# Laying out anew the merge order of eight work streams in a one-core decoder-layer kernel

## The reference

```python
x = layernorm(x + attn(x, Wqkv, Wo))                 # 16 heads of 128, 2 kv heads, rotary,
                                                     # 30*tanh(logits/30), causal, softmax, @ Wo
x = layernorm(x + xattn(x, ctx, mask, wq..bo))       # 16 heads of 16 against ctx (256 tokens);
                                                     # x and the weights quantised to whole
                                                     # numbers for the q and output projections
x = layernorm(x + ffn(x, Wr, br, W1, W2))            # softmax router, best 4 of 16 blocks of 64,
                                                     # h = gelu(x @ W1.T) * mask; h @ W2.T
```

## Time and profile before

| what | value |
|---|---|
| runs of the kernel | 413.67, 414.06 and 414.71 us, median 414.06 |
| the profiled execution | 413.82 us, its span 412.1 us |
| PE busy | 381.5 us, 93% of the span |
| DVE, ACT, POOL busy | 315.3, 246.8 and 151.4 us |
| granted TensorE clock | 0.998 over the span |

### The profile page before, as it was taken

How to read it: one execution, slowest core, us unless ns; L and a number is a source line. 1 busy time by engine, 2 the same in 40 slices (tenths; PEclk the granted TensorE clock), 3 DMA queues, 4 the chain that set the end, 5 groups by cost and what they waited for, 6 DMA issues and landing times.

```text
span 412.1 us, 9281 instructions
## 1 busy us (share of the span) xinstructions
PE 381.5 (93%) x3144; PEld 327.1 (79%) x3144; DVE 315.3 (77%) x924; ACT 246.8 (60%) x528; POOL 151.4 (37%) x173
## 2 busy tenths in 40 slices
PE   3889899999999989998999999999999989899895
PEld 3768769888899868687898778989869877668794
DVE  4998798367676868888887788688778888777653
ACT  5355642536638894476789356678974256994240
POOL 6488545738645123453422325231113320000101
PEclk9999999999999999999999999999999999999999
DMA  7993435553255313242241612220123000000000
GB/s 224 328 372 107 149 102 150 196 171 92 70 173 162 97 28 77 63 118 78 77 130 41 166 32 46 79 78 25 29 78 104 1 2 14 14 3 2 13 14 27
DMA packets 21134, 38.45 MB, mean 93 GB/s; under 512 B 2528, under 2 KB 11616, under 8 KB 21088
## 3 DMA queue, kind: packets, MB, share of 16 engines
q1 hardware_dynamic: 20272, 37.06, 29.6%
q10 hardware_dynamic: 816, 0.79, 0.6%
HBM read 25.52 MB, written 5.24 MB: 75 GB/s over the span
## 4 chain that ended last, share of the span: by engine, by line
PE 64%; DVE 17%; issue 7%; ACT 6%; POOL 3%; DMA 2%; SPq 0%; DVEq 0%; POOLq 0%; ACTq 0%
PE bank L452 12%; PE acc L539 8%; PE bank L625 6%; PE bank L692 5%; PE bank L677 5%; PE bank L483 5%; PE bank L506 4%; PE bank L614 3%; ACT xs L831 3%; PE bank L565 3%; PE bank L637 2%; PE bank L520 2%; PE bank L491 2%; PE bank L509 2%; DVE wqkv_lo L918 2%
## 5 line engine op out<-in xcount | busy, mean ns | idle before, releaser
L831 ACT ACTIVATE xs<-xs,xneg 128x256 f32<-128x256 f32 x128 | 54.3, 500 | 13.4 <-DVE xneg L1089 13.1
L1248 POOL TENSOR_TENSOR a_lo<-a_flat,a_hi 128x512 fp32r<-128x512 f32 x32 | 41.9, 1311 | 30.2 <-ACT a_flat L752 30.2
L452 PE MATMUL bank<-x_hi,wqkv_hi 128*128 128x256 f32 x144 | 45.6, 317 | 7.3 <-DVE wqkv_lo L918 7.3
L1237 POOL TENSOR_TENSOR q_T<-q_T,rope_s 128x512 f32<-128x512 f32 x24 | 31.1, 1301 | 54.7 <-DMA rope_s<-rope_t 54.4
L539 PE MATMUL acc<-wo_s,a_hi 128*128 128x256 f32 x256 | 50.1, 294 | 1.1 <-POOL a_lo L1248 1.1
L1266 POOL TENSOR_TENSOR rstd<-var_eps,half 128x1 f32<-128x1 f32 x24 | 13.2, 551 | 99.2 <-DVE var_eps L976 99.2
L1089 DVE CUSTOM_DVE_ANT_0 xs<-bank,mask_s 128x256 f32<-128x256 f32 x128 | 46.1, 419 | 1.7 <-PE bank L614 1.6
L506 PE MATMUL bank<-v_s,p_near 128*128 128x129 f32 x256 | 41.6, 277 | 1.5 <-POOL p_far L1255 1.1
L539 PEld LDWEIGHTS acc<-wo_s,a_hi 128*128 128x128 f32 x256 | 39.3, 189 | 3.3 <-POOL a_lo L1248 1.8
L452 PE MATMUL bank<-x_lo,wqkv_hi 128*128 128x256 f32 x144 | 41.3, 287 | 0.0
L452 PE MATMUL bank<-x_hi,wqkv_lo 128*128 128x256 f32 x144 | 41.1, 285 | 0.0
(11 more groups left out here) (152 smaller groups left out, 954.2 us busy)
## 6 DMA issues: line engine op xcount, KB each, us to landing
wo_s<-wo_parts SPq DMA_DIRECT2D x24, 512.0 KB, 3.4
rope_s<-rope_t SPq DMA_DIRECT2D x54, 128.0 KB, 2.3
wo_parts<-wo_s SPq DMA_DIRECT2D x8, 512.0 KB, 3.1
stage<-in_wqkv SPq DMA_DIRECT2D x5, 512.0 KB, 4.5
xs<-in_wo SPq DMA_DIRECT2D x8, 256.0 KB, 3.8
y<-in_x SPq DMA_DIRECT2D x4, 256.0 KB, 2.9
ctx_s<-in_ctxT SPq DMA_DIRECT2D x4, 256.0 KB, 3.1
mask_s<-in_mask SPq DMA_DIRECT2D x4, 256.0 KB, 2.9
```

Source lines behind the costliest of these rows:

```text
L452: ins = mm(ps, lhs[i], rhs[j], start=(k == 0 and n == 0), stop=(last and n == 2))
L831: activation(xs[:, t, m, m2, :], xs[:, t, m, m2, :], ACT.Exp, bias=xneg[:, t, m, m2:m2 + 1], scale=-1.0)\
L1237: g.tensor_tensor(dst, dst, (rope_s if b else rope_t)[:, n % 2], ALU.add).then_inc(sig["rotated", 0], 1)
L1248: g.tensor_tensor(a_lo[:, j % 2], a_flat[:, j % 2], a_hi[:, j % 2].bitcast(F32), ALU.subtract)\
```

## The change: the string ORDER

Only the string changes. Each letter occurs as often as before (m 148, x and y 108 each, s 48, r 45, c 28, n and o 24 each), so each stream has the same operations in the same order, with the same instructions, semaphore waits and buffers; what changes is how the streams are merged.

```diff
 ORDER = (
-    "rrrrrrrmmrsrrssmmrrmsrmmssrmmrsmmmmmmscsmmmmcsmmmrmcmmssmmrrcccmmmmmrrsmmmmmcmssmrrcmmmmmrmmmssmsmrrrmccy"
-    "mssmmmmsxsmmmyxmmxssrmmmxymmmmmmmmxxmymmrrxyxmxxmmmyymsxyyxxxryrxxyyyxxxymyxyyxsxyyxyyyxxssrrymymmmxmyssc"
-    "scmmmxrssxccccrrmmyxmmxsnmmyxmmsxsxymmmxxmmmmxxryxnyrxxnnymmyymmmxxyyymryyxxxyyxyyyxryyroyxxoyymmyxmyxxcc"
-    "ssmmxossrrmmymxsmsmxccnmmmxysrccmoyxoymmyxmsxmnxxymxssxyooyxxxyxxyrxyymxxxnxyyyxxmyxyyymnxyyyyxmyyysyxosy"
-    "xymmmmmmyxmmmmynmmccmmmmnccccynoxoyoxyxnnyxyxoyxyxxoxyxynyxyyyxyxyyyxyxxyxyxxyyxxxoyxnoyxxynnxoyxnonynoon"
-    "onnoooon")
+    "rrrrrrrrmrssmsrmmsrmmmrmssmrrmmmmmrmrsssmmmmmsmmmmsscrmcmmmcmmmmrrccmmmmmmmrrcssmmmmssmrrcmmmmycssmrrmmmm"
+    "mxsssccmmryxmmmmssysrrmmmmmmxmymmyxryymmmmxxymyrrxyxxxmyxxyyymmmmssssyxxxrrxxxxmmmmxyyyxxyyxsysyryxxccmmx"
+    "smmmxxcsysccmmmymxcrrnxmmymmsmmmyssrmyxmmmxnymmrxxmnymmxnyxxxyrrxxyyxmyxoyyroyxxxsxyyymmyxyyxysxymmyxsyy"
+    "xxroycmcnxmyxxccccsssynxroyxmmmmmoyxsmmmxsyoxxysxxxymxxmxmyxxmynrxxxymoxyyyryyxyyxxmyyoyxsyyyssxxmnyyymmx"
+    "mmxmymmymymmcmmycmmmcmxocccyonnonyxxynxnyxyooyyyxxyyxxyxyyxyxxxxyyyyxxxxyyxxxyyoxyxnoxoynnxynxnonyynoon"
+    "onnoonoo")
```

More of the change, by code:

```diff
@@ L135 @@
 ORDER = (
-    "rrrrrrrmmrsrrssmmrrmsrmmssrmmrsmmmmmmscsmmmmcsmmmrmcmmssmmrrcccmmmmmrrsmmmmmcmssmrrcmmmmmrmmmssmsmrrrmccy"
-    "mssmmmmsxsmmmyxmmxssrmmmxymmmmmmmmxxmymmrrxyxmxxmmmyymsxyyxxxryrxxyyyxxxymyxyyxsxyyxyyyxxssrrymymmmxmyssc"
-    "scmmmxrssxccccrrmmyxmmxsnmmyxmmsxsxymmmxxmmmmxxryxnyrxxnnymmyymmmxxyyymryyxxxyyxyyyxryyroyxxoyymmyxmyxxcc"
-    "ssmmxossrrmmymxsmsmxccnmmmxysrccmoyxoymmyxmsxmnxxymxssxyooyxxxyxxyrxyymxxxnxyyyxxmyxyyymnxyyyyxmyyysyxosy"
-    "xymmmmmmyxmmmmynmmccmmmmnccccynoxoyoxyxnnyxyxoyxyxxoxyxynyxyyyxyxyyyxyxxyxyxxyyxxxoyxnoyxxynnxoyxnonynoon"
-    "onnoooon")
+    "rrrrrrrrmrssmsrmmsrmmmrmssmrrmmmmmrmrsssmmmmmsmmmmsscrmcmmmcmmmmrrccmmmmmmmrrcssmmmmssmrrcmmmmycssmrrmmmm"
+    "mxsssccmmryxmmmmssysrrmmmmmmxmymmyxryymmmmxxymyrrxyxxxmyxxyyymmmmssssyxxxrrxxxxmmmmxyyyxxyyxsysyryxxccmmx"
+    "smmmxxcsysccmmmymxcrrnxmmymmsmmmyssrmyxmmmxnymmrxxmmnymmxnyxxxyrrxxyyxmyxoyyroyxxxsxyyymmyxyyxysxymmyxsyy"
+    "xxroycmcnxmyxxccccsssynxroyxmmmmmoyxsmmmxsyoxxysxxxymxxmxmyxxmynrxxxymoxyyyryyxyyxxmyyoyxsyyyssxxmnyyymmx"
+    "mmxmymmymmymmcymmycmmmcmxocccyonnonyxxynxnyxyooyyyxxyyxxyxyyxyxxxxyyyyxxxxyyxxxyyoxyxnoxoynnxynxnonyynoon"
+    "onnoonoo")
 def work_streams():
```

## The result

The new order runs in 399.64 us (four runs, 399.34 to 399.87), the old one on the same chip in 414.38 (four runs, 413.67 to 415.51): ratio 0.9641, 95% interval 0.9617 to 0.9666. The direction was right, the size was not.

A forecast was written before the change was run, and what follows sets the result against it. PE was taken as the busiest engine, with some 40.8 us idle or thin that an order could change; 2.0 (start) + 1.6 (middle) - 0.3 (before last batch) = 3.3 us off 413.82, forecast 410.6, range 405.5 to 416.8.

The forecast's parts named there:

- The start: Up to about 66 us: less PE idle time in the new order, 2.0 us won, bounds 0 to 3.5.
- The walk along the queues: Operation-by-operation timing of the start: proj(0, 0) at 34.7 us, ctx(0, 0) at 61.2, PE idle 7.05 us instead of 9.5.
- Rival 1: POOL limits the start: its 2.0 us are gone, and with the middle halved 413 to 414.5 us; chance 0.16.
- The middle: From 60 us to the last norm1: fewer tight pairs, 1.6 us won, between 4.5 won and 1 lost.
- shortfall of tight pairs: Dense PE work missing between dependent operations against a fixed way through other engines: 5.1 us old, 1.9 new.
- The halving: Only half of the middle's 3.2 us was credited, as a tight pair costs nothing where PE has waited already.
- rival 2: The whole of the middle is won: 2.4 + 4.5 us, giving some 407 us; chance 0.18.
- The stretch before the last batch: 319 to 343 us, DVE without a gap: 0.3 us lost, between 0.7 won and 0.9 lost.
- The end itself: Last 15 operations: one move, ffn(3, t0) ahead of hidden(3, 1, t1), cost 0, at most some 0.3 us.
- Rival 3: DVE falls behind at batch 2's change-over, PE pays 4.3 us or more, 417 us; chance 0.22 with other such bursts.

The follow-up runs named there:

- e1: New order for its first 84 operations, up to the second norm1 of batch 0, then the old order: 410.93 us, ratio 0.9907 to the old kernel.
- e4: Old order with 14 operations moved, most by one to four places, at eleven waits seen in its trace: 413.38 us, ratio 0.9983 to the old kernel.
- e9: Old and new orders merged by position, streams x and y placed as in the new, all others as in the old: 442.93 us, ratio 1.0694.
- e7: New order with three xmix and turn_q(1, 0) moved forward so that their pairs are tight: 409.96 us, ratio 0.9877 to the old kernel.
- e8: Old order with only the move for its largest middle wait, at turn_q(1, 0): 414.16 us, ratio 1.0001 to the old kernel.
- e5: Old order with POOL's a_lo replaced by two writes of about the same time that read nothing: 411.25 us, ratio 0.9923.
- e16: Old order with each cross-attention exponential on ACT done on half its columns: 409.83 us, ratio 0.9890 to the old kernel.
- e14: New order with turn_ox(3, t1) moved ahead of hidden(2, 1, t1) and route(3, t1) ahead of turn_m(3, t0): 400.39 us, ratio 0.9646 to the old kernel.
- e13: Order of e4 given to PE and the bank rotation alone, other engines on the old order: 416.88 us, ratio 1.0041 to the old kernel.
- e2: Old order up to the two norm1 of batch 0, then the new order: 405.14 us, ratio 0.9770 to the old kernel.
- e3: New order up to ctx(2, 1), then the old order: 404.70 us, ratio 0.9759 to the old kernel.
- e11: Old order with six PSUM banks instead of seven: 426.73 us, ratio 1.0272 to the old kernel.
- e12: New order with six PSUM banks instead of seven: 407.92 us, ratio 0.9823 to the old kernel.
- e10: Old and new orders merged by position, streams x and y placed as in the old, all others as in the new: 436.66 us, ratio 1.0533.
- e6: New order with POOL's a_lo replaced by two writes of about the same time that read nothing: 399.81 us, ratio 0.9644 to the old kernel.
- e15: As e14, with near(1, 2) also moved behind val(1) and turn_x(3, t0) ahead of hidden(1, 1, t0): 401.12 us, ratio 0.9663 to the old kernel.

## Why the prediction was right or wrong

**The start: right in mechanism, short by 1 us.** It was forecast at 2.0 us within 0 to 3.5; the lag shows 3.0 at position 66, and e1, which has the new start alone, won 3.8 between medians. The walk along the queues held. PE in order of time, kernel after:

```profile
34.90 0.48 PE L539 MATMUL acc<-wo_s,a_hi 128*128 128x256 f32 x2
...
60.04 1.88 PE L565 MATMUL bank<-wkv_s,ctx_s 128*128 128x512 f32 x4
```

proj(0, 0) was forecast at 34.7 and came at 34.90, where the old order has it at 38.42; `quant_w`, forecast at 46.2, came at 46.54; ctx(0, 0), forecast at 61.2, came 1.2 us sooner. turn(0, 7), put at 14.8 us behind dense work counted from the start of the span, came at 66.37, 12.8 behind (in the old order's trace it is 16.7, where I put 16.1), so what I let go back there (0.8 us behind two `ctx`) did not. Instead 1.1 us go back at near(1, 2), which stands still for POOL's sum at 77.9 us and which my walk did not reach. Rival 1, POOL as the limit of the start, is refuted by the stretch 24 to 38 us: POOL has 12.51 us of work in 14 and PE no gap.

**The middle: this is the step that failed.** "Counted between 60 us and the last `norm1`" the shortfall of tight pairs fell from 5.1 to 1.9 us and I credited 1.6; 9.9 us came, or 11.0 counted up to just ahead of turn_k(3, 0). The halving was not the main fault, since even the full count (4.5 with what hangs on it, rival 2) is less than half. The failed step is that a shortfall, dense work between two operations set against one fixed way for each kind of pair, stood for the time that PE waits. It errs both ways. For the old middle it gives 5.1 us where PE's visible waits alone sum to 7.0 and its lag grows by 14.3. For the new one it leaves 1.9 us, 1.7 of them from `turn` to `proj`, where the trace has no visible wait at all: proj(2, 0), with 2.67 us of dense work where I said that 3.76 were needed, started 3.17 us behind the start of its `turn`, and the lag grew by 0.15 us there.

The measure does not rank orders either: e4 has the smallest shortfall of all and the old order's time, e9 a smaller one than the old and 28.5 us more. What it leaves out is what stands ahead of a pair's work in the queues between. e7 showed 2 us of DVE's other work ahead of a `query`, e8 a norm that stands in DVE's queue for POOL's root, e9 banks held 3.8 and 3.4 us by a reader that was late; by the lag, the part of the collisions that e5 took away is about 1 us of the old middle, and the part of ACT's exponentials that e16 took away about 1.5. My text had the evidence for a larger term: it noted that the waits of the old middle sum to about 10 us, and then let their shortfall of 5 stand for them. The new order leaves PE no visible wait in the middle; that it would do so could not be read from the pairs.

**Single waits do not tell what an order can win.** The prediction costed pair by pair. The traces of e8 and e14 show waits taken away at their place and others in their stead within some microseconds, and the times of e4 and e13 show no gain from 14 moves. e1, e2 and e3 show that whole stretches do keep their gain.

**The stretch before the last batch: right.** turn_k(3, 0) was to stand still for 1.7 us with the later waits shrinking in exchange, 0.3 us lost in all, between 0.7 won and 0.9 lost. PE in order of time, kernel after:

```profile
313.45 0.63 PE L595 MATMUL bank<-ident_s,parts 128*128 128x128 f32 x4 [0.96 <-DVE parts L1047]
```

It waits 0.96 us, and the lag grows by 1.1 us there. From just ahead of it to the end the new order wins about 0.3 us, within the bounds; the 1.4 us of the table leave this loss out, as they start behind it. The end itself was forecast at 0 and is: the last `ffn` to the end takes 4.8 us against 4.7.

**Rival 3, DVE behind at batch 2's change-over, is refuted.** turn_k(2, 0), at 238.2 us, does not wait; the new kernel's PE has 59.00 of 59 us in that stretch. The burst of DVE work that I counted is there, but the operation that it was to hold up is on time; how much slack DVE had when it entered was not read.

**What stays open.** Of the 9.9 to 11 us of the middle, e5 and e16 give two shares in the old order, each by itself: 3.1 for a part of the collisions over the whole kernel (about 1 of it in the middle, by the lag) and about 1.5 for a fifth of ACT's exponentials. They are floors, not the whole of either. The visible waits give 1.0 us to banks and 6.0 to operands; how the rest of the 11 us divides between DVE's queue, POOL's queue and the banks was not separated, and e11 and e12 say only that the old order is the more sensitive to the banks. That the lateness of the queues as a whole made the old middle is thus shown at single places and argued for the sum. A kernel with DVE's work cut without changing its order was not tried.

## What to carry to other kernels

When in-order engines share one merged order, read its worth from the lag of the bottleneck engine behind its own dense work, stretch by stretch, and take as the upper bound of the gain the whole lag that a stretch adds, not the shortfall of its dependent pairs. A pair with nothing between costs (e7), but a loose one may wait as well, as its way is as long as the queues on it, and a wait mended at its place may come back at the next one. Judge a new order as a whole, and walk the queues of all engines for the stretches that bind (the walk of the start was good to about a microsecond in 60). Two orders joined end to end kept the gain of each stretch here (e1, e2, e3); the same two woven together stream by stream cost 5 to 7% (e9, e10).

## What the runs showed of the hardware

- DVE's two-operand add and its cast take 0.43 us alone and 1.30 to 1.38 beside POOL's two-operand sums. The Trainium skill (SBUF — State Buffer, section Who interferes with whom) makes a DVE instruction with two SBUF inputs and a POOL instruction that reads SBUF exclude each other; the durations agree. Beside a write of POOL that reads nothing the add kept its 0.43 us and the cast took 1.07 (e5). At the level of the kernel the part of these collisions that e5 and e6 took away was worth 3.1 us in one order and nothing in the other.
- ACT's exponential of 128x256 takes 500 ns and of 128x128 402, so by estimate about 300 ns of it do not depend on the columns (402 less the 98 that half of them cost).
- With the same head of the program the first matmul came at 6.8 us in most profiles and at 7.9 in some (e1, e2, e11, e12, e15), 1.1 us that belongs to no order. In e3 it came at 6.82, but the second piece of weights kept ACT waiting for 3.68 us where it was 1.68 in the kernel after, and PE stood 2.4 us further behind 45 us of dense work on.
